# Maxima of an attention block from 64 rows, two neighbouring heads in the two halves of the array

## The reference, cut to what matters

```python
c_kv = x @ W_kv_down                                   # 128 latent channels
k_rope = _rotary_apply(c_kv @ W_k_rope, cos, sin)      # 32, the same for all heads
k = (c_kv @ W_k_up).reshape(Bb, Tt, NH, HD)            # 16 heads of 32
v = (c_kv @ W_v_up).reshape(Bb, Tt, NH, HD)
q = (x @ W_q).reshape(Bb, Tt, NH, HD)
q_rope = _rotary_apply(x @ W_q_rope, cos, sin)
scores = jnp.einsum('bqhd,bkhd->bhqk', q, k)
scores = scores + jnp.einsum('bqr,bkr->bqk', q_rope, k_rope)[:, None]
scores = scores / scale                                # sqrt(64)
scores = jnp.where(causal[None, None], -jnp.inf, scores)
w = jax.nn.softmax(scores, axis=-1)
attn = jnp.einsum('bhqk,bkhd->bqhd', w, v).reshape(Bb, Tt, D_MODEL)
```

## Time and profile before

| | before |
|---|---|
| median of three runs | 3626.67 us (3624.75 to 3628.69) |
| span of the profiled execution | 3625.0 us; the profile gives no other time for it |
| TensorE busy (PE) | 97% |
| GpSimd busy (POOL) | 74% |
| VectorE busy (DVE) | 71% |
| weight loads (PEld) | 67% |
| ScalarE busy (ACT) | 50% |

### The profile page before, as it was taken

One profiled execution on the slowest core, in us unless ns is written; L12 is line 12 of the kernel. 1 busy time (PEld: TensorE's weight loads), 2 busy tenths in 40 slices (PEclk: granted clock), 3 DMA queues, 4 the chain that ended last, 5 costly groups with the idle time before them and its releaser, 6 DMA issues. The chain is left out here.

```text
span 3625.0 us, 54216 instructions
## 1 busy us (share of the span) xinstructions
PE 3525.3 (97%) x19552; PEld 2412.3 (67%) x19552; DVE 2566.7 (71%) x5329; ACT 1819.9 (50%) x3455; POOL 2674.0 (74%) x1194
## 2 busy tenths in 40 slices
PE   8999989999999999999999999999999699999999
PEld 4777756666666666666666666666665488888887
DVE  6676777777777777777777777777775466666665
ACT  2434335555555555565555555555555344334443
POOL 2333349889898898888988989889889556666665
PEclk9999989999999999999999999999999899999999
DMA  5789773463634635546346354463551111222220
GB/s 199 267 276 300 260 175 74 105 139 78 134 84 109 137 80 116 116 93 138 82 100 146 78 124 98 96 140 79 114 132 59 62 58 70 70 70 70 70 70 35
DMA packets 232757, 426.58 MB, mean 118 GB/s; under 512 B 25381, under 2 KB 26917, under 8 KB 232489
## 3 DMA queue, kind: packets, MB, share of 16 engines
q1 hardware_dynamic: 232424, 423.10, 44.7%
q10 hardware_dynamic: 64, 0.02, 0.0%
HBM read 300.86 MB, written 121.65 MB: 117 GB/s over the span
## 5 line engine op out<-in xcount | busy, mean ns | idle before, releaser
L1022 ACT ACTIVATE att_probs<-att_ps_s 128x512 f32<-128x512 f32 (+3 forms) x2560 | 1308.1, 536 | 899.4 <-PE att_ps_s L1187 797.4
L1121 POOL TENSOR_TENSOR att_sum_g<-att_sum_g,att_probs 128x2048 f32<-128x2048 f32 (+3 forms) x400 | 1624.4, 4061 | 50.6 <-ACT att_probs L1022 4.8
L1058 DVE TENSOR_REDUCE att_piece_max<-att_ps_m 128x1 f32<-128x512 f32 x1520 | 964.7, 684 | 293.4 <-PE att_ps_m L1170 290.6
L1186 PE MATMUL att_ps_s<-att_q_a,att_k_a 128*128 128x512 f32 (+3 forms) x2560 | 954.2, 377 | 19.9 <-DMA att_q_b<-att_neg_max 9.4
L1187 PE MATMUL att_ps_s<-att_q_b,att_k_b 65*128 65x512 f32 (+3 forms) x2560 | 932.4, 368 | 0.0
L1061 DVE CUSTOM_DVE_ANT_0 att_ps_m<-att_ps_m,mask_qk 128x128 f32<-128x128 f32 x1008 | 478.3, 512 | 268.5 <-PE att_ps_m L1170 256.5
L1170 PE MATMUL att_ps_m<-att_k_a,att_q_a 128*128 128x512 f32 (+3 forms) x1808 | 651.6, 383 | 1.2 <-DVE att_piece_max L1058 0.5
L1186 PEld LDWEIGHTS att_ps_s<-att_q_a,att_k_a 128*128 128x128 f32 x2560 | 485.8, 190 | 171.9 <-issue 67.8
L1193 PE MATMUL att_ps_o<-att_probs,att_v 128*32 128x512 f32 (+3 forms) x5120 | 550.3, 536 | 4.6 <-POOL att_probs L1102 4.1
L1187 PEld LDWEIGHTS att_ps_s<-att_q_b,att_k_b 65*128 65x128 f32 x2560 | 484.6, 189 | 63.2
L1170 PEld LDWEIGHTS att_ps_m<-att_k_a,att_q_a 128*128 128x128 f32 x1808 | 339.2, 191 | 232.3 <-issue 106.5
(11 more groups left out here) (189 smaller groups left out, 4961.8 us busy)
## 6 DMA issues: line engine op xcount, KB each, us to landing
att_q_a<-s_q_hi SPq DMA_DIRECT2D x128, 256.0 KB, 6.3
att_q_a<-s_qr_hi SPq DMA_DIRECT2D x128, 256.0 KB, 7.0
prj_x_sb<-in_x_dram SPq DMA_DIRECT2D x16, 1024.0 KB, 5.3
s_q_hi<-prj_q_hi SPq DMA_DIRECT2D x16, 1024.0 KB, 4.4
s_q_lo<-prj_q_lo SPq DMA_DIRECT2D x16, 1024.0 KB, 6.5
s_k_hi<-prj_k_hi SPq DMA_DIRECT2D x16, 1024.0 KB, 4.8
s_k_lo<-prj_k_lo SPq DMA_DIRECT2D x16, 1024.0 KB, 7.1
s_v<-prj_v_sb SPq DMA_DIRECT2D x16, 1024.0 KB, 9.8
```

Of the source, the lines that this page charges most:

```text
L1022: act.activation(probs[t % RING][:, hh, c0:CH], ps_s[(GH * t + hh) % SBANKS][:, c0:CH], ACT.Exp, scale=SCALE).then_inc(probs_ready, 1)
L1058: dve.tensor_reduce(top, ps_m[:, bank, :], AX_X, ALU.max).then_inc(piece_taken, 1)
L1121: pool.tensor_tensor(sum_g[:, :, c0:CH], sum_g[:, :, c0:CH], new, ALU.add).then_inc(sum_added, 1)
L1186: mm(out[:, c0:CH], k_a[:, hh, i * P:(i + 1) * P], q_a[j][:, hh, c0:CH], start=True, stop=False)
```

## The change

The maxima come from 64 rows only: the high query (with its rotary part) times the high key; the product with the low key is left out of the maxima. The scores themselves keep all their products. An even head uses rows 0 to 63, an odd head rows 64 to 127 (`head_rows`). Queries stand the same in both halves; for odd heads the keys are loaded with their halves exchanged, low parts in rows 0 to 63 and high parts in rows 64 to 127 (`load_key_halves`), which for the scores' first product changes only the order of the rows' terms. For that a key chunk is loaded by eight transfers of two heads each instead of four of four heads.

The order of pieces becomes such that heads 0 and 1, and 2 and 3, of the same block of queries stand next to each other, and everything that deals pieces out moves two at a time. The first of a pair waits for the bank of the second too (`ahead`), with three banks as before. VectorE takes the pieces in the new order.

```diff
--- before.py
+++ after.py
@@ -583,7 +583,7 @@
                     j, *piece = AHEAD[seq]
                     if seq == 0:
                         pe.wait_ge(hf_ready, NC * NCH)
-                        pe.wait_ge(k_in[0], 4 * 16)
+                        pe.wait_ge(k_in[0], 8 * 16)
                         pe.wait_ge(q_in[0], 4 * 16)
                     if seq >= TB:
                         pe.wait_ge(piece_taken, seq - TB + 1)
@@ -594,7 +594,8 @@
                         continue
                     hh, r, kc = piece
                     width = CH if kc < j else (r + 1) * P
-                    mm(ps_t[:, seq % TB, 0:width], q_a[j][:, hh, r * P:(r + 1) * P], k_a[:, hh, kc * CH:kc * CH + width],
+                    rows = head_rows(hh)
+                    mm(ps_t[:, seq % TB, 0:width], q_a[j][rows, hh, r * P:(r + 1) * P], k_a[rows, hh, kc * CH:kc * CH + width],
                        start=True, stop=True).then_inc(piece_ready, 1)
 
             def body(n, nxt):
@@ -688,7 +689,12 @@
 
 def max_pieces(j):
 
-    return [(j, hh, r, kc) for kc in range(j + 1) for hh in range(GH) for r in range(TB)]
+    return [(j, hh, r, kc) for kc in range(j + 1) for two in range(0, GH, 2) for r in range(TB) for hh in (two, two + 1)]
+
+
+def head_rows(hh):
+
+    return slice(2 * HD * (hh % 2), 2 * HD * (hh % 2 + 1))
 
 
 def pieces_ahead():
@@ -720,9 +726,9 @@
     out, seen = {}, 0.0
     for m in pairs:
         for half in (0, 1):
-            done = round(seen)
+            done = 2 * round(seen / 2)
             seen += share(high, m % (NSTEP // 2)) / 2
-            out[2 * m + half] = items[done:round(seen)]
+            out[2 * m + half] = items[done:2 * round(seen / 2)]
     assert sum(map(len, out.values())) == len(items)
     return out
 
@@ -799,11 +805,14 @@
         for row, src in ((0, heads["q_lo"][i]), (HD, rotary("qr_lo", i))):
             sp.dma_start(as_f32(ops["q_b"][j][row:row + HD, :, :]), src).then_inc(ops["qb_in"][j], 16)
 
+    def load_key_halves(dst, i, sem):
+
+        for row, odd, what in ((0, 0, "hi"), (0, 1, "lo"), (2 * HD, 0, "lo"), (2 * HD, 1, "hi")):
+            sp.dma_start(as_f32(dst[row:row + HD, odd:GH:2, :]), heads["k_" + what][i][:, odd:GH:2, :]).then_inc(sem, 16)
+            sp.dma_start(as_f32(dst[row + HD:row + 2 * HD, odd:GH:2, :]), rotary("kr_" + what, i)[:, odd:GH:2, :]).then_inc(sem, 16)
+
     def load_k_a(u, j):
-        i = TCH * u + j
-        for row, src in ((0, heads["k_hi"][i]), (HD, rotary("kr_hi", i)),
-                         (2 * HD, heads["k_lo"][i]), (3 * HD, rotary("kr_lo", i))):
-            sp.dma_start(as_f32(ops["k_a"][row:row + HD, :, j * CH:(j + 1) * CH]), src).then_inc(ops["k_in"][j], 16)
+        load_key_halves(ops["k_a"][:, :, j * CH:(j + 1) * CH], TCH * u + j, ops["k_in"][j])
 
     def load_k_b(u, j):
         i = TCH * u + j
@@ -813,7 +822,7 @@
     def load_v(u, j):
         sp.dma_start(ops["v"][:, j, :, :], scratch["v"][TCH * u + j]).then_inc(ops["v_in"][j], 16)
 
-    return load_q_a, load_q_b, load_k_a, load_k_b, load_v, (heads, rotary)
+    return load_q_a, load_q_b, load_k_a, load_k_b, load_v, load_key_halves
 
 
 def attention(nc, keep, scratch, ops, dram):
@@ -908,17 +917,14 @@
 
         @block.sync
         def _(sp):
-            load_q_a, load_q_b, load_k_a, load_k_b, load_v, (heads, rotary) = operand_loads(sp, scratch, ops, k_b, kb_in)
+            load_q_a, load_q_b, load_k_a, load_k_b, load_v, load_key_halves = operand_loads(sp, scratch, ops, k_b, kb_in)
 
             def load_q(u, j):
                 load_q_a(u, j)
                 load_q_b(u, j)
 
             def load_k_next(u):
-                i = TCH * u
-                for row, src in ((0, heads["k_hi"][i]), (HD, rotary("kr_hi", i)),
-                                 (2 * HD, heads["k_lo"][i]), (3 * HD, rotary("kr_lo", i))):
-                    sp.dma_start(as_f32(k_next[row:row + HD, :, :]), src).then_inc(kn_in, 16)
+                load_key_halves(k_next[:], TCH * u, kn_in)
 
             def place_max(u, j):
                 wait_alone(sp, piece_taken, turned(u, j), sp_mark)
@@ -1146,13 +1152,17 @@
             def loads(u):
                 return 4 * 16 * (u + 1)
 
+            def key_loads(u):
+                return 8 * 16 * (u + 1)
+
             def maximum(item):
 
                 place = PLACE[item]
                 bank = place % MBANKS
                 u, j = item[:2]
-                if place >= MBANKS:
-                    pe.wait_ge(piece_taken, place - MBANKS + 1)
+                ahead = 1 if item[2] != "turn" and item[2] % 2 == 0 else 0
+                if place + ahead >= MBANKS:
+                    pe.wait_ge(piece_taken, place + ahead - MBANKS + 1)
                 if item[2] == "turn":
                     pe.wait_ge(max_ready, LAST.index((u, *max_pieces(j)[-1])) + 1)
                     pe.transpose(ps_m[0:GH * TB, bank, 0:P], row_max[:, j, :], keep["ident_f"][:]).then_inc(piece_ready, 1)
@@ -1162,12 +1172,13 @@
                     if kc == 0:
                         pe.wait_ge(q_in[j], loads(u))
                     if from_next(item):
-                        pe.wait_ge(kn_in, 4 * 16 * u)
+                        pe.wait_ge(kn_in, 8 * 16 * u)
                     else:
-                        pe.wait_ge(k_in[kc], loads(u))
+                        pe.wait_ge(k_in[kc], key_loads(u))
                 width = CH if kc < j else (r + 1) * P
-                keys = k_next[:, hh, 0:width] if from_next(item) else k_a[:, hh, kc * CH:kc * CH + width]
-                mm(ps_m[:, bank, 0:width], q_a[j][:, hh, r * P:(r + 1) * P], keys, start=True, stop=True).then_inc(piece_ready, 1)
+                rows = head_rows(hh)
+                keys = k_next[rows, hh, 0:width] if from_next(item) else k_a[rows, hh, kc * CH:kc * CH + width]
+                mm(ps_m[:, bank, 0:width], q_a[j][rows, hh, r * P:(r + 1) * P], keys, start=True, stop=True).then_inc(piece_ready, 1)
 
             def scores(u, j, i, hh):
                 s = FIRST[j] + i
@@ -1180,7 +1191,7 @@
                 if u == 0 and j == 1 and i == 0 and hh == 0:
                     need += [(ones_ready, 2)]
                 if i == TB * j and hh == 0:
-                    need += [(k_in[j], loads(u)), (kb_in[j], 2 * 16 * (u + 1))]
+                    need += [(k_in[j], key_loads(u)), (kb_in[j], 2 * 16 * (u + 1))]
                 waits(pe, *need)
                 out = ps_s[bank]
                 mm(out[:, c0:CH], k_a[:, hh, i * P:(i + 1) * P], q_a[j][:, hh, c0:CH], start=True, stop=False)
@@ -1234,9 +1245,11 @@
                 if t > LAG and t % 2 == 1:
                     parts.append(lambda: [weighted_values(*STEP_OF[due]) for due in (t - LAG - 1, t - LAG)])
                 items = PLAN.get(t, [])
+                sides = sum(it[2] != "turn" for it in items) // 2
+                whole = lambda n: len(items) if n == len(parts) else 2 * (sides * n // len(parts))
                 for n, part in enumerate(parts):
                     part()
-                    for it in items[len(items) * n // len(parts):len(items) * (n + 1) // len(parts)]:
+                    for it in items[whole(n):whole(n + 1)]:
                         maximum(it)
                 if closing and not ENDS_ON_PE[closing[1]]:
                     close_denominators(*closing)
```

## The result

The changed kernel takes 3843.65 us (median of four runs, 3828.08 to 3851.75) against 3627.68 for the kernel before, run again beside it (four runs): a ratio of 1.0592, 95% interval 1.0577 to 1.0608. It is slower, by 216 us; 3775 with a range of 3500 to 3950 was forecast. The profiled execution has a span of 3826.3 us and took 3828.08, the fastest of the four; its granted clock is 0.981, that of the others 0.975 to 0.977, that of the kernel before, whose span is in the earlier trace rows, 0.991.

The account below looks back on a forecast made before the run. TensorE's stream in attention was taken as the bound, GpSimd next. 3627 - 257 (pairs) + 433 (steps) + 3 (pairs ahead of attention) - 30 (waits taken back) = 3776, said as 3775 us; range 3500 to 3950.

Parts of the forecast that it names:

- The pairs stream together: Maxima products in attention: the two of a pair run at once, so half of 513 us goes, -257 us.
- The steps: TensorE in attention: each change between full and half height costs 0.20 us, 2167 of them, +433 us.
- the quarters: Products in quarters of the columns on TensorE: stepping into them costs about 0.22 us, out 0.11; four stream together.
- the one 4-row transpose: The step from 128-row to 4-row transposes on TensorE: the first comes 0.09 us late, evidence that row changes cost.
- rival C's first half: Second load of a pair queues behind the first, +134 us; C, with binding banks as alternative: 3910, chance 0.15.
- B: Steps on TensorE cost emptying alone, 3565 us, or only one direction costs, 3587, up to 3690; chance 0.20.
- A: Pairs on TensorE stream together at free steps: faster, 3467 us (3430 to 3500); chance 0.20.
- D: The halves on TensorE don't stream together at all: 4030 us; chance 0.03.
- The forecast for the scores behind the pair: Profile sign: scores follow 0.5 to 0.55 us from the pair's start instead of 0.23.
- What waits took back: Slower TensorE in attention finds exponentials and maxima ready: of 77 + 89 us of waits, -30 us, between 0 and 60.
- Three banks, two taken at once: Pairs waiting for VectorE to free maxima banks: no more waiting than before; +125 us if the banks bind.
- The loads: Eight key transfers instead of four, some 1.9 us more on SyncE: cost nothing; 30 us if cover were gone.

Follow-up runs that it names:

- the full-height version: The changed kernel with its order, bank waits and eight transfers, but each product of a maximum over all 128 rows again: 3718.63 us, ratio 1.0250.
- the light maxima: VectorE reduces only the first 128 columns of each piece, same edit in the changed kernel and the kernel before: 3729.31 and 3598.75 us.

## Why the prediction was right, and where it was off

**The bound.** TensorE's stream was the bound and stayed it: drawn as busy for 97% of attention, and what was added to it came out in the time.

**The pairs stream together** (-257 us): shown. Their products and loads are drawn at one time. The Trainium skill, TensorE: Matmul & The Clock Gate, Part 3, gives some 4 ns between the starts of tiles that run at once; the trace agrees, with less than 0.01 us.

**The steps** (2167 x 0.20 = 433 us): shown in place, and in size in the timeline; in end time they are 0.17 to 0.18 us each. The guess from the quarters and from the one 4-row transpose held; 64 columns, which step freely, were no guide to 64 rows. The Trainium skill, TensorEngine Tiling (Array Packing), Key Properties, has a drain at each change of tiling mode; the trace agrees for rows, with 0.09 and 0.11 us. The products of 64 columns lose nothing, and whether they change the mode at all no row says. In the timeline a pair adds what was worked out, 0.09 + 0.11 before it and 0.11 + 0.11 behind. The second load of a pair does not queue (rival C's first half falls), emptying alone is not the price (B falls), the steps are not free (A falls), and the halves do stream together (D falls). The forecast for the scores behind the pair, 0.50 to 0.55, holds for their stream (0.44 until they are drawn and 0.11 for their load).

**What waits took back** (-30 us): mis-sized, but inside its 0 to 60. At full clock the steps cost (7.3 + 16.0) x 16 = 373 us of end time and not 433, so 60 came back, the upper end.

**Three banks, two taken at once** (nothing): this is the term that failed. The prediction had "I take it as no more than before" and priced it at +125 only for the case that the banks bind. They do: the full-height version, which has nothing else, is 91 us slower, 65 of them by the wait of the first for both banks. In the changed kernel, whose pairs lie further apart, it is (157.4 - 146.7 - 7.3) x 16 = 54 us by the units at full clock, and 85 by the light maxima, which take the first unit and the clock with them. The prediction set the 1.1 to 1.5 us between pairs against VectorE's 1.4 and called it enough, and looked for the waits in steps with six pieces; but pairs with one head between them stand at the lower end, 1.1, and most of them wait. Its sign was load waits under 150 us, and 462 (291 + 171) are drawn; some 200 of these are steps that name VectorE, so this sign was badly chosen, and the time is the better measure.

**The clock** (nothing): not foreseen. The units that are longer than the rest and the first one account for most of what is left. In the profiled execution: 16 x 10.7 = 171 of 200 us are in the unit at full clock; the first unit has 16.4 more than that (198.9 against 171.8 before), the middle ones 19 together, and the last one 6 less. The other 15 us up to the median are between this execution and the slower three, whose clock is lower. Three things speak for the clock as the cause. The amounts fit: what the mean clock leaves out is 0.019 x 3826 = 73 us here and 0.009 x 3625 = 33 before, 40 more. Of the 19 us, 16 or 17 are in the five units with stretches at 1.2 GHz. And with light maxima there is no such stretch in any middle unit, and they stay within 1 us. No run takes the clock away by itself.

In sum, by the units: steps less saving 117, banks 54, clock and the ends of the stage 30, and 15 between the executions: 216. The forecast had 146 + 3 for the first and nothing for the others: it took the steps 32 us too dear and left out 99. So the direction and the larger term rest on a mechanism that the runs show, but that 3843.65 lies in the narrower 3700 to 3850, too, is in part luck: it was meant for banks that do not bind and a clock that stays, and the two errors cancel by a third. **The loads** cost nothing: shown.

## What to carry to other kernels

Here two matmuls in the two halves of the array's rows really run at once, but a step between full and half height costs about 0.2 us each way, nearly a whole 512-column product, so by this sum half height could pay only where several pairs stand between two steps; the one run of that kind was lost to its score banks. Count the steps, not the products. A wait for two banks of three leaves a single piece of slack to the engine that empties them: run the pairing with full products first, as it shows that cost alone. And an engine that is named as what ended an idle time may have been done long before: compare with its own row, or take its work away, as with the light maxima.

## What was not expected of the hardware

The clock falls in a TensorE that is drawn as busy. The kernel before has a mean granted clock of 0.991, the changed kernel 0.981 to 0.975, and with 2106 separate half-height groups 0.899, though TensorE is drawn as busy for 97 to 98% of the span in these. The full-height version with the same order has 0.990. Fewer rows alone do not say when: with light maxima the same 1263 groups of half height leave all middle units at 1.00. And the control with two score banks, all at full height, has stretches at 1.2 GHz in six of its fourteen middle units, at 0.99 and 154.5 us against 152.9. In these runs it falls in middle units where waits come on top of steps, where waits for exponentials are many, and where the steps are most; what decides it is not shown. The start of attention in the kernel after (columns as in the earlier trace rows), and a short fall later:

```profile
474.00:520.00 46.00, 38.64 (x117) 18.06 (x121) 20.70 (x54) 11.74 (x24) 10.89 (x8) 0.54 0.82 169
...
975.00:983.00 8.00, 7.25 (x43) 3.39 (x42) 6.13 (x18) 3.75 (x9) 6.44 (x4) 1.00 0.58 127
983.00:987.00 4.00, 3.90 (x22) 2.52 (x26) 3.41 (x7) 1.51 (x6) 3.33 (x3) 0.83 0.03 13
```

In the first 46 us the clock is 0.54; before the change it was 0.82 there. At 985.6, by the trace's record of the clock, TensorE falls to 1.2 GHz, after it had waited 0.70 us for a bank at 982.96 and made scores of 256 and 128 columns with pairs between them:

```profile
982.96 0.49 PE L1181 MATMUL att_ps_m<-att_k_a,att_q_a 64*128 64x512 f32 x2 [0.70 <-DVE att_piece_max L1064]
984.24 0.51 PE L1181 MATMUL att_ps_m<-att_k_a,att_q_a 64*128 64x512 f32 x2
984.67 0.33 PE L1197 MATMUL att_ps_s<-att_q_a,att_k_a 128*128 128x128 f32 x1
...
985.28 0.28 PE L1198 MATMUL att_ps_s<-att_q_b,att_k_b 65*128 65x128 f32 x1
985.52 0.71 PE L1181 MATMUL att_ps_m<-att_k_a,att_q_a 64*128 64x512 f32 x2
986.16 0.47 PE L1197 MATMUL att_ps_s<-att_q_a,att_k_a 128*128 128x128 f32 x1
```

The scores of 128 columns behind the pair at 985.52 come after 0.64 us, those behind the pair at 984.24 after 0.43.
